# Score stacks interleaved over the partitions, branch 1's loads at other heads, blank rows copied from a constant

## What is computed

```
xn = _layernorm(x, axis=-1)
x = x + _L0_attn_ref(xn, ...) + _L0_ffn_ref(xn, ...)
xn = _layernorm(x, axis=-1)
x = x + _L1_attn_ref(xn, ...) + _L1_ffn_ref(xn, ...)

# both attentions of layer 1, 16 heads of 16 columns, 512 rows:
scores = einsum('bhqd,bhkd->bhqk', q, k)
scores = where(causal, scores, -inf)
probs = softmax(scores, axis=-1)
attn = einsum('bhqk,bhkd->bhqd', probs, v)
# experts: top_k of 2, cw holds their softmax, y the expert outputs
moe = einsum('eth,te->th', y, cw)
```

## Time and profile before

| | us |
|---|---|
| three runs: median (lowest to highest) | 675.85 (674.94 to 676.86) |
| the profiled execution | 679.32 |
| its span, first to last instruction | 677.5 |
| busy in it: PE / DVE / ACT / POOL | 570.8 / 476.2 / 309.1 / 220.6 |
| chain that ended last: PE, DVE, DMA, POOL | 36%, 9%, 6%, 4% |
| of it DMA `Qs<-mT` / `pieces<-P` | 2% / 1% |

### The profile page before, as it was taken

The page is one execution under the profiler, slowest core; times in us unless marked ns, Lnnn a source line. Parts: engine busy times, 40 slices in busy tenths (PEclk is TensorE's granted clock), DMA queues, the critical chain, the costliest instruction groups (busy, mean ns, idle before and its releaser), DMA issues.

```text
span 677.5 us, 10978 instructions
## 1 busy us (share of the span) xinstructions
PE 570.8 (84%) x3694; PEld 409.3 (60%) x3694; DVE 476.2 (70%) x1054; ACT 309.1 (46%) x569; POOL 220.6 (33%) x229
## 2 busy tenths in 40 slices
PE   1777789889578999989699988897978789999990
PEld 1634367668367888874355554464544578888870
DVE  5789976797775467759468678768782477677753
ACT  2647322313322333550456545544546556665640
POOL 2667546646553533772200010010044011211120
PEclk9989889989698999995889999999999899999995
DMA  5221100000220008399944331500025892000005
GB/s 176 83 82 61 60 0 1 1 0 17 77 75 16 1 1 199 101 217 279 164 80 84 62 71 26 95 2 2 2 89 219 326 372 89 25 31 25 24 32 194
DMA packets 32876, 58.61 MB, mean 87 GB/s; under 512 B 6838, under 2 KB 24662, under 8 KB 30262
## 3 DMA queue, kind: packets, MB, share of 16 engines
q1 hardware_dynamic: 30566, 52.58, 29.0%
q0 software_dynamic: 1872, 5.13, 2.1%
q10 hardware_dynamic: 384, 0.20, 0.1%
HBM read 42.10 MB, written 15.51 MB: 85 GB/s over the span
## 4 chain that ended last, share of the span: by engine, by line
PE 36%; DVE 9%; DMA 6%; POOL 4%; issue 3%; ACT 1%; SPq 1%; ACTq 0%; POOLq 0%; DVEq 0%
PE bank L834 19%; PE bank L828 4%; DVE small L1825 3%; PE bank L1097 3%; PE bank L1074 3%; PE bank L1047 3%; DMA Qs<-mT 2%; DMA sorted_rows<-rows,slot_i 2%; POOL sorted_rows L2281 1%; DMA pieces<-P 1%; PE bank L1076 1%; PE bank L1049 1%; DMA rows<-sorted_rows 1%; SPq L729 1%; PE bank L1114 1%
## 5 line engine op out<-in xcount | busy, mean ns | idle before, releaser
L1825 DVE TENSOR_REDUCE small<-bank 128x1 f32<-128x256 f32 (+3 forms) x256 | 107.7, 483 | 15.9 <-PE bank L1049 14.9
L1047 PE MATMUL bank<-Ks,Qs 96*128 96x256 bf16 (+3 forms) x256 | 66.6, 328 | 8.3 <-DVE small L1825 6.9
L2087 DVE TENSOR_TENSOR wl<-wall,wh 128x1024 fp32r<-128x1024 f32 x46 | 56.2, 1222 | 22.7 <-ACT wh L1526 20.7
L1074 PE MATMUL bank<-Qs,Ks 99*128 99x512 bf16 (+3 forms) x256 | 59.8, 309 | 7.1 <-DMA Qs<-mT 4.6
L1380 ACT ACTIVATE PTb<-bank 128x512 f32<-128x512 f32 (+1 forms) x96 | 43.7, 529 | 34.6 <-PE bank L1076 31.8
L1380 ACT ACTIVATE PTa<-bank 128x512 f32<-128x512 f32 (+1 forms) x96 | 43.5, 529 | 33.0 <-PE bank L1076 27.9
L1074 PEld LDWEIGHTS bank<-Qs,Ks 99*128 99x128 bf16 x256 | 25.5, 100 | 50.5 <-issue 23.6
L1049 PE MATMUL bank<-maskb,identb 128*128 128x128 bf16 x256 | 55.3, 235 | 0.0
L1331 ACT ACTIVATE sg<-bank 128x512 f32<-128x512 f32 (+1 forms) x28 | 16.8, 598 | 70.2 <-PE bank L834 70.1
L1526 ACT CAST wh<-wall 128x1024 fp32r x46 | 48.0, 1044 | 1.6 <-issue 0.3
L1076 PE MATMUL bank<-identb,maskb 128*128 128x128 bf16 x256 | 47.8, 224 | 0.0
(11 more groups left out here) (359 smaller groups left out, 1525.9 us busy)
## 6 DMA issues: line engine op xcount, KB each, us to landing
wall<-e_pack SPq DMA_DIRECT2D x8, 1536.0 KB, 9.6
Qs<-pieces SPq DMA_DIRECT2D x48, 128.0 KB, 5.9
stg<-w_pack SPq DMA_DIRECT2D x18, 256.0 KB, 2.8
pieces<-P SPq DMA_DIRECT2D x9, 512.0 KB, 9.1
wf<-t_pack SPq DMA_DIRECT2D x12, 256.0 KB, 2.7
Ks<-pieces SPq DMA_DIRECT2D x8, 384.0 KB, 5.4
sorted_rows<-blank SPq DMA_DIRECT2D x1, 2944.0 KB, 13.4
Ks<-pieces SPq DMA_DIRECT2D x8, 256.0 KB, 5.1
```

Source lines behind the costliest of these rows:

```text
L1047: nc.tensor.matmul(banks[b][:, o:o + w], Q[0:96, h, i * P:(i + 1) * P], K[0:96, h, 0:w], start=True, stop=False)
L1074: nc.tensor.matmul(banks[b][:, o:o + w], K[0:99, h, j * P:(j + 1) * P], Q[0:99, h, j * P:CH], start=True, stop=False)
L1825: last = nc.vector.tensor_reduce(mxv[:, i, h:h + 1], banks[b][:, o:o + w], AX.X, ALU.max, negate=True)
L2087: nc.vector.tensor_tensor(weight_part("l", i, half), wall[:, bass.ds(place + half * KC * EI, KC * EI)], weight_part("h", i, half).bitcast( ...
```

## The change

`STACK_Q` and `STACK_K` become plain lists of parts, one for each of six pairs. `stack` loads pair i's 16 rows to partitions i, i + 6, ..., i + 90, K and Q in turn, so each call issues four transfers of 128 KB and a half has 12; the wait of the scores counts 12. Branch 1's loads are let go by heads 9, 11, 13 and 15, 17, 19. The first quad's exponentials wait only for the pieces whose tile `PTa` covers, the second's for the other two. The blank rows come from a new input of the program, copied from HBM to HBM by one transfer that SP issues after the centring matrix; `blank`, `spare` and the three GpSimd instructions that set them are gone.

```diff
-STACK_Q = [(0, 0, 1), (16, 0, 1), (32, 0, 1), (48, 1, 1), (64, 1, 1), (80, 2, 1)]
-STACK_K = [(0, 0, 3), (48, 0, 2), (80, 0, 1)]
+STACK_K = (0, 1, 2, 0, 1, 0)
+STACK_Q = (0, 0, 0, 1, 1, 2)
...
-                    g = (4 + 6 * half + 2 * j) if n == 1 else H * (n - 1) + 8 * half + 2 * j
+                    g = (9 + 6 * half + 2 * j) if n == 1 else H * (n - 1) + 8 * half + 2 * j
...
-            for dst, blk, (row, part, parts) in ((K, 2, STACK_K[j]), (Q, 0, STACK_Q[2 * j]), (Q, 0, STACK_Q[2 * j + 1])):
-                src = pieces[n, blk + half, part:part + parts].rearrange("c (r h) t -> (c r) h t", h=8)
-                sp.dma_start(dst[row:row + HD * parts, h0:h1, :], src).then_inc(s_stack[n % 2][half], 16)
+            for i in (2 * j, 2 * j + 1):
+                for dst, blk, part in ((K, 2, STACK_K[i]), (Q, 0, STACK_Q[i])):
+                    src = pieces[n, blk + half, part].rearrange("(r h) t -> r h t", h=8)
+                    sp.dma_start(dst[i:6 * HD:6, h0:h1, :], src).then_inc(s_stack[n % 2][half], 16)
...
             sp.dma_start(L0["wf"][:, 0, :], c_pack[:, o:o + CENTRE]).then_inc(s_centre, 16)
+            spread = lambda t: t.rearrange("(p b) d -> p (b d)", p=P)
+            sp.dma_start(spread(sorted_rows), spread(blank_pack)).then_inc(s_blank, 16)
...
-            sp.wait_ge(*blank_set.upto("rows"))
-            by_block = sorted_rows.rearrange("(b p) d -> p b d", p=P)
-            sp.dma_start(by_block[:, :, 0:D], L1["blank"][:].unsqueeze(1).broadcast_to([P, BLOCKS, D])).then_inc(s_blank, 16)
-            sp.dma_start(by_block[:, :, D:ROW], L1["spare"][:]).then_inc(s_blank, 16)
...
-                    pe.wait_ge(s_stack[n % 2][h // 8], 9 * 16 * (n // 2 + 1))
+                    pe.wait_ge(s_stack[n % 2][h // 8], 12 * 16 * (n // 2 + 1))
...
+                    elif q == 0:
+                        act.wait_ge(*p_l.upto(N_TILES - 1))
+                        act.wait_ge(s_pw[PN[2]], 48)
                     else:
-                        act.wait_ge(*p_l.upto(N_TILES - 1))
-                        for n in PN[1:4]:
+                        for n in (PN[1], PN[3]):
                             act.wait_ge(s_pw[n], 48)
...
-                    nc.gpsimd.memset(L1["blank"][:], 0.0).then_inc(*blank_set.tick("zero"))
-                    nc.gpsimd.memset(L1["spare"][:], 0.0).then_inc(*blank_set.tick("shares"))
-                    pool.wait_ge(*blank_set.upto("shares"))
-                    nc.gpsimd.iota(L1["spare"][:, :, 1].bitcast(I32), [[P, BLOCKS]], base=2 * NT * P, channel_multiplier=1)\
-                        .then_inc(*blank_set.tick("rows"))
...
-                    pool.wait_ge(s_blank, 32)
+                    pool.wait_ge(s_blank, 16)
```

More of the change, by code:

```diff
@@ L105, in upto, with build @@
         return self.sem, self.order.get(key, 1)
-def build(nc, orders, w_pack, t_pack, c_pack, r_pack, e_pack, vec_pack, bias_pack, x_in, out):
+def build(nc, orders, w_pack, t_pack, c_pack, r_pack, e_pack, vec_pack, bias_pack, blank_pack, x_in, out):
     from contextlib import ExitStack
@@ L216, in build @@
                         ("Osb", [CH], F32), ("mtok", [TPC, 12], BF16), ("mT", [2, CH], BF16),
-                        ("route", [sum(n for _, n in ROUTE)], F32), ("blank", [D], F32), ("choice", [NT, 2], F32),
+                        ("route", [sum(n for _, n in ROUTE)], F32), ("choice", [NT, 2], F32),
                         ("share", [2, NT], F32), ("hot", [2, NE, NT], F32), ("both", [NE * NT], F32),
@@ L226, in build @@
         pta, o = plan([("PTa", [4, 1280], F32)], mlp_at)
-        l1d, o = plan([("spare", [BLOCKS, 2], F32), ("ranks", [6, NE], F32), ("by_rank", [NE, NE], F32), ("load_i", [NE], I32),
+        l1d, o = plan([("ranks", [6, NE], F32), ("by_rank", [NE, NE], F32), ("load_i", [NE], I32),
                        ("places", [2, BLOCKS], F32), ("place_i", [BLOCKS], I32), ("ones_row", [CH], BF16)], o)
@@ L2363, in constants @@
     r_pack = np.concatenate([route[n] for n, _ in ROUTE], 1).astype(np.float32)
-    return c_pack, r_pack
+    blank = np.zeros((BLOCKS * P, ROW), np.int32)
+    blank[:, D + 1] = 2 * NT * P + np.arange(BLOCKS * P)
+    return c_pack, r_pack, blank.view(np.float32)
 def kernel(**inputs):
@@ L2371 @@
     w_pack, t_pack, e_pack, vec, bias = pack_inputs(inputs)
-    c_pack, r_pack = constants(np.asarray(inputs["L1_ffn_w_ln2"]))
+    c_pack, r_pack, blank = constants(np.asarray(inputs["L1_ffn_w_ln2"]))
     arrays = {"w_pack": w_pack, "t_pack": t_pack, "c_pack": c_pack, "r_pack": r_pack, "e_pack": e_pack, "vec_pack": vec,
-              "bias_pack": bias, "x_in": np.asarray(inputs["L0_attn_x"])}
+              "bias_pack": bias, "blank_pack": blank, "x_in": np.asarray(inputs["L0_attn_x"])}
     arrays = {k: np.ascontiguousarray(v) for k, v in arrays.items()}
```

## The result

| kernel | ratio to before (95% interval) | median us, before beside it |
|---|---|---|
| the change | 0.9917 (0.9896 to 0.9938) | 672.27, 677.79 |
| the change, measured again beside experiments | 0.9880 (0.9845 to 0.9914) | 671.23, 679.38 |

The kernel is faster by 5.6 us in the first comparison and by 8.2 in the second. Forecast was a gain of 7.49 us and 668.4, with a range of 666.9 to 672.4. The 672.27 lies just under the top of that range, and 5.6 us are three quarters of the gain forecast. So the number was about right.

What follows compares the result with a forecast made beforehand. Transfer queues that never run empty were taken to make TensorE wait for `mT` near 332 us. Gains of 4.65 + 0.37 + 2.47 = 7.49 us take the median 675.85 to 668.4 us, range 666.9 to 672.4.

Steps and rivals of the forecast that it cites:

- First term: TensorE's idle time before its restart at 336.85 us, waiting for the `mT` transfers, goes entirely: 4.65 us gained.
- the clock term: TensorE's slow clock after the `mT` wait goes with that wait: 2.47 us gained, bounds 0 and 2.47.
- The bounds of the weave: Woven stack loads run between 150 GB/s (old rate) and 298 (SP's issue); the last `mT` lands between 327 and 329 us.
- Second term: ScalarE's table load for the first exponentials starts earlier, after waiting for branch 1's `pieces` alone: 0.37 us gained.
- the foot of the range: 666.9 us, 1.5 us below the forecast, if the clock is also high in the 3.6 us before 331.9.
- Third term: From 336.85 to 342.39 us TensorE's granted clock of 0.50 rises once the idle time goes: 2.47 us gained.
- Head 16: Its stack lands at 340.0 us, its scores start at 340.6: margin 0.6 us, wait taken as 0.
- blank rows: Dropping the write at 258 to 270 us gains 0; the copy, done by 88 us, costs 0, bound 1 us.
- C: Head 16 finds its stack landing 10.8 us after issue, 6.0 us late; 674.4 us, no change; chance 0.08.
- D: Woven rows load slowly, slower kernel below 87 GB/s; at 75 head 8 is 15.1 us late, 683.5 us; chance 0.06.
- E: Cut loads each pay a cost in turn, 12 taking 14.0 us; head 8 waits 1.2 us, 669.6 us; chance 0.04.
- B: Wait goes, part is given back: slow clock stays (670.8 us) or head 16 waits 1 to 3 us (669.5 to 671.4); chance 0.28.

## Why the prediction was right in size and wrong in its cause

The sum was worked out for the heads, with the weave at 0 us, and it is the weave that brings it in. That the total fits is to this extent luck: whatever keeps the queue ahead of `mT` short frees the same wait and the same clock.

**First term, 4.65 us: right in size, given to the wrong part.** Take the profiled pair and count from the 1.7 us that the changed kernel was ahead. Before the transposed scores of head 4 it is 1.2 us further ahead; at them 4.9 more.

**But the step behind it failed.** I wrote that the last `mT` part lands in time at either bound, 150 or 298 GB/s, and that a weave that speeds up nothing "would change nothing in the sum". For quad 1 this is nearly so: no wait with heads alone, 1.22 us in the change without the weave. What I missed is quad 3: the text itself gives 210 GB/s for the groups of heads 15 to 20, "above the old rate", and holds this only against the stack's due time at head 24. The `mT` of quad 3 goes through the same queues, is wanted by head 20, and has no such margin. With heads alone, TensorE waits for it 2.87 us, and the clock term comes back too. The 3.6 us that the same kernel loses at the first quad stand in no term either. The heads move the crowd; the weave removes it. That the heads were what mattered is refuted by the change with heads 4 and 10: 0.9885.

**The bounds of the weave.** Both were badly read. The 150 GB/s of the earlier trace rows were a mixture, with K loads of 48 and 32 rows among those of 16; where all loads are of 16 adjacent rows they run at 107 to 132. The sentence that the trace shows more than the Trainium skill's 104 GB/s rested on that mixture. The upper bound took 0.44 us an issue from transfers to adjacent rows; strided ones cost SP 0.59, with a gap 0.63 apart, so 128 KB in 0.63 us, 208 GB/s. The true rate, held by SP, lies between the bounds, and the path it opens was not priced: I put the weave at 0 us, and it is worth all of the gain. I had quoted the nearer rate and let the row overrule it without asking what the row averaged.

**Second term, 0.37 us: wrong.** After the common 1.7 us the table load comes 0.15 us later, not 0.37 earlier. It now waits for transposed scores, and these start at 319.07 after 0.40 us of idle time. The `mT` issue of quad 0 takes ScalarE 3.75 us (2.41 before) while the queues are still full, and the last of its single transfers runs at 318.31, so its landing is the likely cause; no run isolates it. ScalarE's rows, first of the change, then of the kernel before:

```profile
312.41 3.75 ACTq L1483 DMA_DIRECT2D Qs<-mT  x3
...
319.87 1.28 ACT L1381 ACT_TABLE_LOAD   x1 [7.49 <-PE bank L1075]
```

```profile
314.13 2.41 ACTq L1482 DMA_DIRECT2D Qs<-mT  x3
```

With the wait alone split, the load came 0.1 us earlier. The 1.2 us ahead of head 4, found with the first term, are the clock between 325 and 329, at 1.00; I had put this into the foot of the range only.

**Third term, 2.47 us: the step is right, the size 1.9.** From head 4's row to head 5's it took 5.54 us before and takes 3.63 now, at a clock of 1.00.

**Head 16, blank rows, rivals.** Head 16 didn't wait; the last group goes out at 334.36, lands some 2.7 later, and is wanted at 338.35. The blank copy costs nothing that could be measured, with VectorE busy 14.00 of 14.00 us beside it:

```profile
66.00:80.00 14.00, 10.95 (x54) 5.98 (x54) 14.00 (x21) 5.42 (x9) 7.42 (x7) 0.88 0.83 285
```

C and D did not come; D's danger is the kernel with adjacent rows, where the loads did come too slowly. E is refuted by the landing of 2.6 us: cutting costs nothing here if the rows are spread. (With adjacent rows the 12 loads of the first half, 1.57 MB, do fill the 13 us from 288 to 301, nearly E's 14.0.) B came in another place: of 9.7 us ahead from 345 to 480, the changed kernel keeps 5.0 at 530 and 7.4 at the end. The loss is the clock: about 1.5 us go at each of the first two stretches below and 1.7 at the third, and 2.4 come back where the kernel before has a clock of 0.76, from 530 to 537. The changed kernel's stretches, then two of the weave alone:

```profile
484.00:488.00 4.00, 3.88 (x21) 1.46 (x22) 3.64 (x15) 0.57 (x1) 0.74 (x1) 0.57 0.03 10
...
497.00:501.00 4.00, 4.00 (x33) 2.85 (x32) 1.85 (x5) 2.05 (x4) 0.42 (x1) 0.58 0.90 253
...
521.00:525.00 4.00, 3.63 (x25) 1.27 (x29) 0.38 (x1) 0.12 (x1) 0.00 (x0) 0.57 1.06 437
```

```profile
484.00:488.00 4.00, 2.45 (x26) 1.13 (x24) 3.69 (x16) 1.94 (x4) 0.00 (x0) 1.00 0.02 6
...
521.00:525.00 4.00, 3.00 (x36) 1.37 (x36) 0.27 (x2) 0.59 (x1) 0.00 (x0) 1.00 1.02 353
```

In every kernel TensorE is idle for 1.55 us at the place of the program that stands just ahead of the first of these stretches, waiting for VectorE's routing; after it the clock fell in the change (in both its profiles), with heads 4 and 10 again and with the blank rows alone, and in no other kernel. All three have the blank copy, but four kernels with the copy kept their clock there (the weave undone, adjacent rows, 32 partitions, six transfers). So no one part accounts for it, and why it falls in one and not in the other stays open. The 1.5 us are about the difference between the change and the weave alone.

## What to carry to other kernels

A transfer that writes few rows should write them far apart: the same 128 KB landed in 2.6 us over every sixth partition and in 11.5 over adjacent ones, both from 280 to 305 us. When a backlog is moved, look at every small transfer that shares the queue, quad by quad, and not just at the data that the backlog carries. And before a rate from a stretch is taken as a bound, ask which shapes it averages: here it hid that the smallest shape ran some 12 to 29% slower.

## What the hardware showed that I had not expected

- Spreading pays at a reach of 32 partitions already: 213 GB/s at a share of 0.76, and 3.0 us to landing, against 11.5 us for neighbours.
- The price of a stride lies with SP: 0.59 us an issue against 0.42, whatever the reach.
- A source read three times moved at a share of 0.19, three sixteenths, and the one read twice at 0.13, two. The Trainium skill's "DMA: Bandwidth & Descriptors", section "Why a DMA increments its semaphore by 16 and not by 1", says that a copy goes to the largest number of engines up to 16 that divides the outer dimensions of both sides, which for a triple and 48 rows is 3. The trace agrees.
